# Wk's sums on VectorE late in the first chunk, and the next heads' operands earlier in the second pass

## The chip, the cores and the metric

The kernel runs on one core of a Trainium2 chip. The metric is the device time of one execution in microseconds. The kernel before has a median of 1039.54 us over three runs (1039.32, 1039.54, 1044.28).

## What is computed

A pre-norm layer on 2048 tokens of 512 features, in float32: a linear attention with 32 heads of 64, then a mixture of 8 experts with top 2.

```python
xn = layernorm(x)
q = relu(xn @ Wq); k = relu(xn @ Wk); v = xn @ Wv          # 512 -> 2048, 32 heads of 64
kv = einsum('bhsd,bhse->bhde', k, v)
key_sum = k.sum(over tokens)
out = (q @ kv) / clip(q @ key_sum, 1e-6)                   # per head
x = x + out @ Wo + bo
xn2 = layernorm(x)                                         # experts: H = 352
x = x + sum over the token's 2 best experts of gate * (silu(xn2 @ w1.T + b1) @ w2.T + b2)
```

## The kernel before

**Precision.** Each float32 matmul is three matmuls (`three`, lines 1928 to 1930) on operands split in a high and a low part: ScalarE casts the high part, VectorE subtracts it from the source for the low part (`lo`, line 1373). A product is ready for TensorE only when both have been made. Every engine runs its own queue in the order in which it is written, and engines wait for each other through semaphores; a waiting instruction holds all behind it on its engine.

**K projection and accumulation.** v is never projected. The kernel builds A^T = xn^T k (512 x 2048, in four chunks of 512 columns of k, `NC`), over 16 token tiles (`NT`), in the PSUM banks `pA`. K tiles come from `pK`. `kacc` collects k's sum over tokens.

- *First chunk* (tiles n = 0 to 15): per tile TensorE projects k of the next tile (12 matmuls, `project_k`), transposes one tile of xn, and accumulates (12 matmuls, `accumulate_at`). VectorE and ScalarE meanwhile do layernorm, the splits of xn, its transpose xnT and k, and one split of Wk a step (`split_wk`, table `WK_SPLIT`). `wk_in`, `wk2_in` and `t_raw` are staging areas in SBUF of four 512-column units each.
- *Groups* (g = 0 to 7): chunks 1 and 2 of k, for two tiles at a time, come from seven products instead of eight (the Winograd form of Strassen's scheme), from sums of Wk's quarters and sums of xnT's halves. Wk's sums (eight units of 128x512) are made once: by GpSimd in four instructions of 128x1024 (lines 662 to 668). The sums of xnT are `raw_sum`, split by `sum_hi` and `sum_lo`; the first group's stand ahead of `act_group` and `dve_group`, behind chunk 0. Chunk 2's k is stored to HBM as `k2`.
- *Second pass* (j = 0 to 7): k2 is loaded again and accumulated for chunk 2, two accumulations a turn. Between them lies the work of one pair of heads j: `pe_kv(j)` multiplies A^T's block (`at_hl`) with Wv, and `pe_m(j)` the block-diagonal of the result (`bd_hi`, `bd_lo`) with Wo. Their operands come from `act_operands` and `act_pair` on ScalarE (wv_hi, wo_hi, at_hl, ks_hl), `pool_operands` on GpSimd (wv_lo, wo_lo) and `dve_pair` on VectorE (low halves of at_hl and ks_hl). TensorE's turn: `pe_kv(j)`, accumulation of tile 2j-1 of k2, `pe_m(j)`, accumulation of tile 2j. `put_at(1)` copies chunk 1's finished A^T out of `pA` in turn 0; the second accumulation of that turn waits for it (`at_act`, `at_dve`).
- *Loads in the second pass* go through SyncE's one queue, in this order for pairs 4 to 7: k2 tile 2n, k2 tile 2n+1, Wv and Wo of pair n. The load of k2 tile i waits until the sum of tile i-4 (`kacc_done`) frees its buffer; Wk's last chunk (1 MB) goes ahead of pair 3.
- Then chunk 3 runs like chunk 0 (`pe_chunk`), the q projection and output product follow, and the experts.

Of the kernel before, what the change touches and what calls it, by code (L numbers as in the profile page):

```python
# [67 lines left out]
def block_kernel(nc, x, Wq, Wk, Wv, Wo, bo, gate_w, gate_b, gbias, w1, b1, w2, b2, out):  # L68
# [171 lines left out]
    with ExitStack() as ctx:  # L240
# [169 lines left out]
        WK_SPLIT = tuple((n, n + 2) for n in range(2, 14))  # L410
        wk_units = lambda n: [u for m, u in WK_SPLIT if m == n]
# [35 lines left out]
        def _(sp):  # L447
# [4 lines left out]
            for g in range(4):  # L452
# [5 lines left out]
                if g == 0:  # L458
# [6 lines left out]
            sp.dma_start(wk2_in[:, :].rearrange("p (f n) -> p f n", f=FB),  # L465
                         Wk[:, 2 * CW:3 * CW].rearrange("(f p) n -> p f n", p=P)).then_inc(s_wk, 16)
            sp.wait_ge(wk_lo_ready, FB)
            load_wk(1)
            def load_wq(c):
# [165 lines left out]
        def _(pool):  # L635
# [23 lines left out]

            two = lambda a, h: a[:, 2 * h * CW:2 * (h + 1) * CW]  # L660
            pool.wait_ge(s_wk, 32)
            pool.tensor_tensor(two(t_raw, 0), two(wk2_in, 0), two(wk_in, 0), ALU.subtract).then_inc(t_step, 1)
            pool.wait_ge(t_step, 1)
            pool.tensor_tensor(two(t_raw, 1), two(wk2_in, 1), two(t_raw, 0), ALU.subtract).then_inc(t_step, 1)
            pool.tensor_tensor(two(wk2_in, 0), two(wk2_in, 1), two(wk2_in, 0), ALU.subtract).then_inc(t_step, 1)
            pool.wait_ge(t_step, 3)
            pool.wait_ge(wk_lo_ready, 2 * FB)
            pool.tensor_tensor(two(wk_in, 1), two(t_raw, 1), two(wk_in, 1), ALU.subtract).then_inc(t_step, 1)
# [211 lines left out]
        def _(act):  # L880
            def split_wk(u, n):
                if n < FB:
                    act.wait_ge(s_block[n], 16)
                elif n >= 4 * FB + 2:
                    act.wait_ge(s_wk, 48)
                else:
                    act.wait_ge(s_wk, 32)
                    if u < 2 or u >= 10:
                        act.wait_ge(t_step, 4 if u < 2 else u // 2 - 4)
# [66 lines left out]
            def split_k2(i):  # L956
# [3 lines left out]
                else:  # L960
                    act.wait_ge(s_block[i % 4], 16 * (i // 4 + (1 if i % 4 < 2 else 2)))
# [27 lines left out]
            for n in range(NT):  # L989
                if n > 0:  # L990
                    split_k(n, n % 2)
                for u in wk_units(n):
                    split_wk(u, u)
                if n + 1 < NT:
                    act.wait_ge(xn_ready, n + 2)
# [71 lines left out]
            def act_group(g):  # L1067
# [3 lines left out]
                right_hi(g)  # L1071
                sum_hi(g, 4)
                if g > 0:
                    split_xn(n, 2 * g, 0)
# [16 lines left out]
            for k in (2, 1, 3):  # L1091
                sum_hi(0, k)
# [5 lines left out]
            for j in range(8):  # L1098
# [4 lines left out]
                act_bd(j)  # L1103
# [1324 lines left out]
```

## Time and profile before

| | |
|---|---|
| profiled execution, its own time | 1038.22 us |
| its span, first to last instruction | 1036.2 us |
| median of three timed runs | 1039.54 us |
| TensorE (PE) busy | 994.3 us, 96% |
| VectorE (DVE) busy | 745.3 us, 72% |
| ScalarE (ACT) busy | 518.4 us, 50% |
| GpSimd (POOL) busy | 289.0 us, 28% |

Busy shares are over the whole span, and TensorE's count overlapping matmuls, so its gaps must be looked for in a timeline. The page also cuts the span in 40 slices of 26 us; TensorE's row reads

```profile
PE   9899899997769999999999999999999989999998
```

in tenths, so that the only low stretch is slices 10 to 12 (233 to 311 us), in the second pass. Chunk 0 runs from the start to some 113 us, the groups to 234 us, the second pass to 319 us.

### The profile page before, as it was taken

Reading aid. Unit: us, or ns where it says so; the run is one execution under the profiler, and the core shown is the slowest. Engines: PE = TensorE matmul, PEld = TensorE weight load, DVE = VectorE, ACT = ScalarE, POOL = GpSimd, SP = SyncE. Lnnn points to the kernel's source line nnn. Section 1 sums busy time; section 2 is a strip of 40 time slices with the busy share of each in tenths; the row PEclk is TensorE's granted clock in tenths of the full one; section 3 lists DMA queues with packets and bytes.
Section 4 is the critical chain, followed back from the end, with each engine's and each line's share of the span. In section 5 each row is a group of like instructions: output and inputs, shape, how many; then the busy total and the mean of one; then the engine's idle time right before and its main releaser. Section 6 shows DMA issues by size and latency. Waiting matters only on the chain.

```text
span 1036.2 us, 17405 instructions
## 1 busy us (share of the span) xinstructions
PE 994.3 (96%) x4981; PEld 831.3 (80%) x4982; DVE 745.3 (72%) x1646; ACT 518.4 (50%) x1354; POOL 289.0 (28%) x433
## 2 busy tenths in 40 slices
PE   9899899997769999999999999999999989999998
PEld 7678688886657888888788888888888879899896
DVE  7988787877786566766788787887887665444453
ACT  4445423335554455865555555555555863434342
POOL 1210000012230000230432223322233555655554
PEclk9999999999999999999999999999999999999999
DMA  8000500104231003233212111111204735555553
GB/s 296 1 0 12 213 28 34 41 21 142 92 91 62 21 21 122 82 115 127 80 42 42 50 41 50 42 51 47 45 31 159 212 115 100 102 104 101 102 113 47
DMA packets 50898, 82.76 MB, mean 80 GB/s; under 512 B 6537, under 2 KB 19002, under 8 KB 50722
## 3 DMA queue, kind: packets, MB, share of 16 engines
q1 hardware_dynamic: 41042, 63.38, 19.3%
q0 software_dynamic: 9808, 18.79, 9.7%
q8 instruction: 24, 0.39, 0.2%
q14 instruction: 24, 0.20, 0.1%
HBM read 56.81 MB, written 27.17 MB: 81 GB/s over the span
## 4 chain that ended last, share of the span: by engine, by line
PE 85%; DVE 8%; ACT 5%; issue 1%; DMA 1%; SPq 0%; POOL 0%; ACTq 0%; DVEq 0%; POOLq 0%
PE pK L1928 15%; PE pK L1930 15%; PE pK L1929 15%; PE pX L1928 5%; PE pX L1930 5%; PE pX L1929 5%; PE pA L1928 5%; PE pA L1930 5%; PE pA L1929 5%; PE pA L2132 3%; PE pT L2342 2%; PE pT L2010 2%; PE pX L2360 1%; DVE ks_hl L1373 1%; DVE at_hl L1556 1%
## 5 line engine op out<-in xcount | busy, mean ns | idle before, releaser
L1139 ACT ACTIVATE qs<-q,nrec 128x64 f32<-128x64 f32 x512 | 129.6, 335 | 88.9 <-DVE nrec L1658 86.4
L657 POOL TENSOR_TENSOR wv_lo<-wv_in,wv_hi 128x512 fp32r<-128x512 f32 x12 | 15.4, 1287 | 354.5 <-ACT wo_hi L1010 354.5
L1928 PE MATMUL pA<-k_hi,xn_hi 128*128 128x512 f32 x256 | 101.5, 396 | 0.9 <-DVE k_lo L1393 0.6
L1928 PE MATMUL pK<-wq_hi,xnT_hi 128*128 128x512 f32 x256 | 100.4, 392 | 0.0
L1929 PE MATMUL pA<-k_lo,xn_hi 128*128 128x512 f32 x256 | 100.0, 391 | 0.0
L1930 PE MATMUL pA<-k_hi,xn_lo 128*128 128x512 f32 x256 | 99.9, 390 | 0.0
L1930 PE MATMUL pK<-wq_hi,xnT_lo 128*128 128x512 f32 x256 | 99.9, 390 | 0.0
L1929 PE MATMUL pK<-wq_lo,xnT_hi 128*128 128x512 f32 x256 | 99.7, 389 | 0.0
L1928 PE MATMUL pX<-m_hi,qsT_hi 128*128 128x512 f32 x240 | 99.1, 413 | 0.0
L1930 PE MATMUL pX<-m_hi,qsT_lo 128*128 128x512 f32 x240 | 94.2, 392 | 0.0
L1929 PE MATMUL pX<-m_lo,qsT_hi 128*128 128x512 f32 x240 | 93.7, 390 | 0.0
L1651 DVE TENSOR_TENSOR qs<-q,ksum 128x512 f32<-128x512 f32 x64 | 52.9, 827 | 54.5 <-ACT q L1133 54.5
L791 POOL DMA_INDIRECT out<-y,slot_token x38 | 65.9, 1733 | 69.4 <-DVE y L1894 42.3
L1928 PE MATMUL pK<-wk_hi,xnT_hi 128*128 128x512 f32 x192 | 76.3, 397 | 6.4 <-DVE xnT_lo L1373 3.9
L1929 PE MATMUL pK<-wk_lo,xnT_hi 128*128 128x512 f32 x192 | 74.9, 390 | 0.0
L1930 PE MATMUL pK<-wk_hi,xnT_lo 128*128 128x512 f32 x192 | 74.9, 390 | 0.0
L1133 ACT ACTIVATE q<-pK 128x512 f32<-128x512 f32 x64 | 38.1, 596 | 67.5 <-PE pK L1930 67.5
L1315 ACT ACTIVATE hT<-pX,b1T 128x128 f32<-128x128 f32 (+1 forms) x117 | 34.0, 362 | 72.0 <-PE pX L2360 64.1
L912 ACT CAST xn_hi<-xn 128x512 fp32r<-128x512 f32 x64 | 39.5, 617 | 50.8 <-PE pA L1930 50.8
L1928 PEld LDWEIGHTS pA<-k_hi,xn_hi 128*128 128x128 f32 x256 | 48.3, 189 | 11.5 <-DVE xn_lo L1373 0.8
L1373 DVE TENSOR_TENSOR gT_lo<-pT,gT_hi 128x512 fp32r<-128x512 f32 x39 | 27.0, 691 | 41.7 <-ACT gT_hi L1301 41.7
L1373 DVE TENSOR_TENSOR xn_lo<-xn,xn_hi 128x512 fp32r<-128x512 f32 x64 | 46.1, 720 | 14.9 <-ACT xn_hi L912 14.9
(314 smaller groups left out, 2603.0 us busy)
## 6 DMA issues: line engine op xcount, KB each, us to landing
w_in<-in_ffn_w SPq DMA_DIRECT2D x22, 256.0 KB, 3.6
w_in<-in_ffn_w SPq DMA_DIRECT2D x8, 704.0 KB, 7.2
xn<-in_attn_hidden_states SPq DMA_DIRECT2D x16, 256.0 KB, 6.3
wv_in<-in_attn_Wv SPq DMA_DIRECT2D x16, 256.0 KB, 2.9
wo_in<-in_attn_Wo SPq DMA_DIRECT2D x16, 256.0 KB, 3.1
xnT_dram<-xnT SPq DMA_DIRECT2D x4, 1024.0 KB, 9.6
wk_in<-in_attn_Wq SPq DMA_DIRECT2D x4, 1024.0 KB, 6.1
x_in<-in_attn_hidden_states SPq DMA_DIRECT2D x16, 256.0 KB, 2.6
```

The costliest lines, as they stand in the source:

```text
L791: pool.indirect_dma_start(out, bass.IndirectOffsetOnAxis(slot_token[:, i:i + 1].bitcast(U32), 0), rows, None, bounds_check=T - 1, oob_is_e ...
L912: nc.scalar.copy(xn_hi[:, b * D:(b + 1) * D], xn[:, ds(t * D, D)]).then_inc(xn_hi_ready, 1)
L1133: nc.scalar.activation(q[:, b * CW:(b + 1) * CW], pK[:, b * 512:(b + 1) * 512], ACT.Relu).then_inc(q_ready, 1)
L1139: i = nc.scalar.activation(qs[:, s], q[:, s], ACT.Copy, scale=nrec[:, b * HC + h:b * HC + h + 1])
L1315: last = nc.scalar.activation(hT[0:w, b * P:(b + 1) * P], pX[0:w, b * P:(b + 1) * P], ACT.Silu, bias=b1T[0:w, ds(b * E + e, 1)])
L1373: return nc.vector.tensor_tensor(dst, src, f(hi), ALU.subtract)
L1651: nc.vector.tensor_tensor(qs[:, b * CW:(b + 1) * CW], q[:, b * CW:(b + 1) * CW], ksum[:, c * CW:(c + 1) * CW], ALU.mult).then_inc(qk_ready, 1)
L1928: nc.tensor.matmul(dst, lhs[0], rhs[0], start=start, stop=False)
L1929: nc.tensor.matmul(dst, lhs[0], rhs[1], start=False, stop=False)
L1930: return nc.tensor.matmul(dst, lhs[1], rhs[0], start=False, stop=stop)
L2010: nc.tensor.matmul(pT[:, 0:256], w[:, b * D + i * P:b * D + (i + 1) * P], at_hl[:, i * 256:(i + 1) * 256], start=i == 0 and w is wv_hi, st ...
L2132: i = nc.tensor.transpose(pA[:, (2 + b) * 512 + j * P:(2 + b) * 512 + (j + 1) * P], qs[:, b * CW + j * P:b * CW + (j + 1) * P], ident[:, :])
```

## The change

In the first chunk GpSimd's four instructions go. VectorE makes the eight sums, 128x512 each, in `wk_sum`, by a table `WK_SUMS` of (step, sum): one at steps 8, 9 and 12, three at 13, two at 14. The table `WK_SPLIT` of (step, unit) changes with it: up to step 7 as before, then units 10 and 11 at steps 10 and 11, 12 and 13 at step 13, 14 and 15 at step 14. SyncE loads chunk 1 of Wk ahead of chunk 2, which now reports to `s_block[0]`. The first group's sums are made at step 15 of the first chunk, ahead of the split of xn's tile 16, and `right` and sum 4 with them. In the second pass the operands of pair j+1 are made on ScalarE and VectorE directly behind bd of pair j, ahead of `put_at(1)` and of the splits for the turn's other accumulation.

```diff
@@ -407,8 +407,9 @@
             at_ = (e * HB + hb) * D
             return bank[0:w], w, w2_to[0:w, at_:at_ + D]
 
-        WK_SPLIT = tuple((n, n + 2) for n in range(2, 14))
-        wk_units = lambda n: [u for m, u in WK_SPLIT if m == n]
+        WK_SPLIT = ((2, 4), (3, 5), (4, 6), (5, 7), (6, 8), (7, 9), (10, 10), (11, 11), (13, 12), (13, 13), (14, 14), (14, 15))
+        WK_SUMS = ((8, 0), (9, 1), (12, 2), (13, 3), (13, 4), (13, 5), (14, 6), (14, 7))
+        at_step = lambda table, n: [u for m, u in table if m == n]
 
         def wk_raw(u):
             if u < 2:
@@ -462,10 +463,10 @@
             sp.dma_start(bo_b[:, :], bo.partition_broadcast(P)).then_inc(s_small, 16)
             sp.dma_start(gb_b[:, :], gate_b.partition_broadcast(P)).then_inc(s_small, 16)
             sp.dma_start(gb2_b[:, :], gbias.partition_broadcast(P)).then_inc(s_small, 16)
-            sp.dma_start(wk2_in[:, :].rearrange("p (f n) -> p f n", f=FB),
-                         Wk[:, 2 * CW:3 * CW].rearrange("(f p) n -> p f n", p=P)).then_inc(s_wk, 16)
             sp.wait_ge(wk_lo_ready, FB)
             load_wk(1)
+            sp.dma_start(wk2_in[:, :].rearrange("p (f n) -> p f n", f=FB),
+                         Wk[:, 2 * CW:3 * CW].rearrange("(f p) n -> p f n", p=P)).then_inc(s_block[0], 16)
             def load_wq(c):
                 sp.dma_start(wk_in[:, :].rearrange("p (f n) -> p f n", f=FB),
                              Wq[:, c * CW:(c + 1) * CW].rearrange("(f p) n -> p f n", p=P)).then_inc(s_wq[c], 16)
@@ -657,16 +658,6 @@
                 pool.tensor_tensor(wv_lo[:, b], wv_in[:, b], f(wv_hi[:, b]), ALU.subtract).then_inc(wv_lo_ready, 1)
                 pool.tensor_tensor(wo_lo[:, b], wo_in[:, b], f(wo_hi[:, b]), ALU.subtract).then_inc(wo_lo_ready, 1)
 
-            two = lambda a, h: a[:, 2 * h * CW:2 * (h + 1) * CW]
-            pool.wait_ge(s_wk, 32)
-            pool.tensor_tensor(two(t_raw, 0), two(wk2_in, 0), two(wk_in, 0), ALU.subtract).then_inc(t_step, 1)
-            pool.wait_ge(t_step, 1)
-            pool.tensor_tensor(two(t_raw, 1), two(wk2_in, 1), two(t_raw, 0), ALU.subtract).then_inc(t_step, 1)
-            pool.tensor_tensor(two(wk2_in, 0), two(wk2_in, 1), two(wk2_in, 0), ALU.subtract).then_inc(t_step, 1)
-            pool.wait_ge(t_step, 3)
-            pool.wait_ge(wk_lo_ready, 2 * FB)
-            pool.tensor_tensor(two(wk_in, 1), two(t_raw, 1), two(wk_in, 1), ALU.subtract).then_inc(t_step, 1)
-
             for n in (*range(NPOOL), *range(NP - 4, NP)):
                 pool_operands(n)
 
@@ -882,11 +873,13 @@
                 if n < FB:
                     act.wait_ge(s_block[n], 16)
                 elif n >= 4 * FB + 2:
-                    act.wait_ge(s_wk, 48)
+                    act.wait_ge(s_wk, 32)
+                elif 4 <= u < 8:
+                    act.wait_ge(s_wk, 16)
+                elif u in (8, 9):
+                    act.wait_ge(s_block[0], 32)
                 else:
-                    act.wait_ge(s_wk, 32)
-                    if u < 2 or u >= 10:
-                        act.wait_ge(t_step, 4 if u < 2 else u // 2 - 4)
+                    act.wait_ge(t_step, u + 7 if u < 2 else u - 9)
                 src = wk_in[:, u % FB * CW:(u % FB + 1) * CW] if n < FB or n >= 4 * FB + 2 else wk_raw(u)
                 nc.scalar.copy(wk_hi[:, u * CW:(u + 1) * CW], src).then_inc(wk_hi_ready, 1)
 
@@ -958,7 +951,7 @@
                 if i < 2:
                     act.wait_ge(k2_ready, 2 * NG)
                 else:
-                    act.wait_ge(s_block[i % 4], 16 * (i // 4 + (1 if i % 4 < 2 else 2)))
+                    act.wait_ge(s_block[i % 4], 16 * (i // 4 + (1 if i % 4 == 1 else 2)))
                 act.wait_ge(a_done, n - 1)
                 nc.scalar.activation(k_hi[:, i % 2 * CW:(i % 2 + 1) * CW], k2_of(i), ACT.Relu).then_inc(k_hi_ready, 1)
 
@@ -989,8 +982,13 @@
             for n in range(NT):
                 if n > 0:
                     split_k(n, n % 2)
-                for u in wk_units(n):
+                for u in at_step(WK_SPLIT, n):
                     split_wk(u, u)
+                if n == NT - 1:
+                    for k in (2, 1, 3):
+                        sum_hi(0, k)
+                    right_hi(0)
+                    sum_hi(0, 4)
                 if n + 1 < NT:
                     act.wait_ge(xn_ready, n + 2)
                 split_xn(n + 1, (n + 1) % NT, (n + 1) % 2)
@@ -1068,9 +1066,9 @@
                 n = NT + 2 * g
                 if g > 0:
                     split_c(n - 1)
-                right_hi(g)
-                sum_hi(g, 4)
                 if g > 0:
+                    right_hi(g)
+                    sum_hi(g, 4)
                     split_xn(n, 2 * g, 0)
                 act.wait_ge(prod_done, 7 * g + 1)
                 nc.scalar.copy(p1[:, :], pK[:, 0:512]).then_inc(p1_ready, 1)
@@ -1088,8 +1086,6 @@
                     for k in (2, 1, 3):
                         sum_hi(g + 1, k)
 
-            for k in (2, 1, 3):
-                sum_hi(0, k)
             for u in range(2):
                 split_wk(u, 4 * FB + u)
             for g in range(NG):
@@ -1101,16 +1097,16 @@
                 split_xn(n, tile2(2 * j), 0)
                 act_part(j)
                 act_bd(j)
+                if j == 3:
+                    at_ready(2)
+                if j < 7:
+                    act_operands(j + 1, (j + 1) % 2, 32 * ((j + 1) // 2) + 32)
+                    act_pair(j + 1, (j + 1) % 4)
                 if j == 0:
                     put_at(1)
                 split_k2(2 * j + 1)
                 split_xn(n + 1, tile2(2 * j + 1), 1)
                 act_m(j)
-                if j == 3:
-                    at_ready(2)
-                if j < 7:
-                    act_operands(j + 1, (j + 1) % 2, 32 * ((j + 1) // 2) + 32)
-                    act_pair(j + 1, (j + 1) % 4)
                 if 3 <= j < 7:
                     split_wk(NT - 7 + j, 4 * FB + j - 1)
                 if j == 6:
@@ -1412,6 +1408,21 @@
             def sub(out, a, b, op=ALU.subtract):
                 return nc.vector.tensor_tensor(out, a, b, op)
 
+            def wk_sum(i):
+                if i == 0:
+                    dve.wait_ge(s_wk, 16)
+                    dve.wait_ge(s_block[0], 32)
+                dve.wait_ge(t_step, i)
+                if i == 6:
+                    dve.wait_ge(wk_lo_ready, 2 * FB)
+                unit = lambda a, n: a[:, n * CW:(n + 1) * CW]
+                h = i % 2
+                out, a, b = ((unit(t_raw, h), unit(wk2_in, h), unit(wk_in, h)),
+                             (unit(t_raw, 2 + h), unit(wk2_in, 2 + h), unit(t_raw, h)),
+                             (unit(wk2_in, h), unit(wk2_in, 2 + h), unit(wk2_in, h)),
+                             (unit(wk_in, 2 + h), unit(t_raw, 2 + h), unit(wk_in, 2 + h)))[i // 2]
+                sub(out, a, b).then_inc(t_step, 1)
+
             left = lambda t: xnT[:, t * D:t * D + HALF]
             right = lambda t: xnT[:, t * D + HALF:(t + 1) * D]
 
@@ -1456,9 +1467,8 @@
                 if g > 0:
                     split_c(n - 1)
                     add_k(1, n - 1, 1)
-                right_lo(g)
-                sum_lo(g, 4)
-                if g > 0:
+                    right_lo(g)
+                    sum_lo(g, 4)
                     split_xn(n, 2 * g, 0)
                 dve.wait_ge(prod_done, 7 * g + 2)
                 dve.wait_ge(p1_ready, g + 1)
@@ -1535,8 +1545,20 @@
                 if n > 0:
                     split_k(n, n % 2)
                     add_k(0, n, n % 2)
-                for u in wk_units(n):
+                for u in at_step(WK_SUMS, n):
+                    wk_sum(u)
+                for u in at_step(WK_SPLIT, n):
                     split_wk(u, u)
+                if n == NT - 1:
+                    for k in (1, 2):
+                        raw_sum(0, k)
+                    sum_lo(0, 2)
+                    sum_lo(0, 1)
+                    raw_sum(0, 3)
+                    raw_sum(0, 4)
+                    sum_lo(0, 3)
+                    right_lo(0)
+                    sum_lo(0, 4)
                 split_xn(n + 1, (n + 1) % NT, (n + 1) % 2)
                 if n + 2 < NT:
                     split_xnT(n + 2, n + 2, n % 2)
@@ -1604,13 +1626,6 @@
                             dve_m(pair)
                 put_at(c)
 
-            for k in (1, 2):
-                raw_sum(0, k)
-            sum_lo(0, 2)
-            sum_lo(0, 1)
-            raw_sum(0, 3)
-            raw_sum(0, 4)
-            sum_lo(0, 3)
             for u in range(2):
                 split_wk(u, 4 * FB + u)
             for g in range(NG):
@@ -1624,14 +1639,14 @@
                 add_k2(2 * j)
                 dve_kvT(j)
                 dve_bd(j)
+                if j < 7:
+                    dve_pair(j + 1, (j + 1) % 4, (j + 1) % 2)
                 if j == 0:
                     put_at(1)
                 split_k2(2 * j + 1)
                 split_xn(n + 1, tile2(2 * j + 1), 1)
                 add_k2(2 * j + 1)
                 dve_m(j)
-                if j < 7:
-                    dve_pair(j + 1, (j + 1) % 4, (j + 1) % 2)
                 if 3 <= j < 7:
                     split_wk(NT - 7 + j, 4 * FB + j - 1)
                 if j == 6:
```

## Rows read from the trace of the kernel before

**Rows 1.** Who TensorE waited for, whole span: total us, times, longest.
```profile
PE pT L2010 <- DVE ks_hl L1373: 18.8, 8, 2.7
```
**Rows 2.** Timeline of GpSimd, 22 to 60 us: start, duration, instruction, idle before.
```profile
26.47 2.41 POOL L662 TENSOR_TENSOR t_raw<-wk_in 128x1024 f32<-128x1024 f32 x1 [22.88 <-DMA wk_in<-in_attn_Wk]
...
51.74 2.69 POOL L668 TENSOR_TENSOR wk_in<-t_raw,wk_in 128x1024 f32<-128x1024 f32 x1 [17.56 <-DVE wk_lo L1373]
```
**Rows 3.** Timeline of VectorE, 22 to 60 us.
```profile
31.88 2.85 DVE L1373 TENSOR_TENSOR xn_lo<-xn,xn_hi 128x512 fp32r<-128x512 f32 x1
...
52.28 2.69 DVE L1373 TENSOR_TENSOR xnT_lo<-xnT,xnT_hi 128x512 fp32r<-128x512 f32 x1
```
**Rows 4.** Timeline of TensorE, 22 to 76 us: transposes of three tiles.
```profile
22.69 0.60 PE L1943 MATMUL pT<-ident,xn 128*128 128x128 f32 x4
...
69.97 0.60 PE L1943 MATMUL pT<-ident,xn 128*128 128x128 f32 x4
...
75.89 0.60 PE L1943 MATMUL pT<-ident,xn 128*128 128x128 f32 x4
```
**Rows 5.** Timeline of VectorE, 98 to 116 us.
```profile
100.20 0.68 DVE L1373 TENSOR_TENSOR wk_lo<-wk_in,wk_hi 128x512 fp32r<-128x512 f32 x1
...
109.69 0.42 DVE L1413 TENSOR_TENSOR s_raw<-xnT 128x256 f32<-128x256 f32 x1
110.14 0.42 DVE L1413 TENSOR_TENSOR s_raw<-s_raw,xnT 128x256 f32<-128x256 f32 x1
```
**Rows 6.** Timeline of TensorE and ScalarE, 102 to 116 us.
```profile
102.79 0.39 PE L1928 MATMUL pK<-wk_hi,xnT_hi 128*128 128x512 f32 x1
...
114.38 0.57 ACT L1076 COPY p<-pK 128x512 f32<-128x512 f32 x1
...
115.09 0.47 PE L1928 MATMUL pK<-wk_hi,s_hi 128*128 128x512 f32 x1 [1.26 <-DVE xnT_lo L1373]
```
**Rows 7.** Timeline of VectorE, second pass, turns 0, 1 and 7.
```profile
237.71 0.28 DVE L1564 TENSOR_TENSOR ksum<-pT,part 128x128 f32<-128x128 f32 x1
...
239.24 1.29 DVE L1409 COPY at<-pA 128x512 f32<-128x512 f32 x2
...
243.26 1.16 DVE L1556 TENSOR_TENSOR at_hl<-at,at_hl 128x512 fp32r<-128x512 f32 x1 [0.21 <-ACT ks_hl L1014]
...
245.62 0.68 DVE L1507 SCALAR_TENSOR_TENSOR k_lo<-k_in,k_hi 128x512 fp32r<-128x512 f32 x1
...
251.87 0.69 DVE L1513 SCALAR_TENSOR_TENSOR kacc<-k_in,kacc 128x512 f32<-128x512 f32 x1
...
311.49 0.28 DVE L1564 TENSOR_TENSOR ksum<-pT,part 128x128 f32<-128x128 f32 x1
```
**Rows 8.** Timeline of ScalarE, second pass, turn 0.
```profile
238.75 1.07 ACT L924 COPY at<-pA 128x512 f32<-128x512 f32 x2
...
241.37 0.62 ACT L1009 CAST wv_hi<-wv_in 128x512 fp32r<-128x512 f32 x1
```
**Rows 9.** Timeline of TensorE: turn 0, m(7), and chunk 3's first projection.
```profile
240.63 0.47 PE L1928 MATMUL pA<-k_hi,xn_hi 128*128 128x512 f32 x1 [0.34 <-issue]
...
313.13 0.47 PE L1928 MATMUL pX<-wo_hi,bd_hi 128*128 128x512 f32 x1 [0.98 <-DVE bd_lo L1373]
...
319.37 0.39 PE L1928 MATMUL pK<-wk_hi,xnT_hi 128*128 128x512 f32 x1
```
**Rows 10.** Timeline of SyncE's queue: the Wo load of pair 3.
```profile
253.98 0.50 SPq L477 DMA_DIRECT2D wo_in<-in_attn_Wo  x1
```
**Rows 11.** DMA issues, 253.8 to 256 and 264.8 to 265.5 us: KB, us to landing.
```profile
wo_in<-in_attn_Wo SPq DMA_DIRECT2D x1, 256.0 KB, 5.8
...
wo_in<-in_attn_Wo SPq DMA_DIRECT2D x1, 256.0 KB, 3.7
```
**Rows 12.** Busy time by stretch: length, PE, PEld, DVE, ACT, POOL, granted clock, DMA, GB/s.
```profile
254.00:256.00 2.00, 0.02 (x1) 0.05 (x1) 2.00 (x3) 0.53 (x2) 1.69 (x2) 0.93 0.97 288
256.00:258.00 2.00, 2.00 (x9) 2.00 (x10) 1.64 (x3) 0.00 (x0) 0.00 (x0) 0.50 1.05 384
```

## The prediction

> **What bounds the kernel now.** I read the page's busy shares first: TensorE is nearly always busy, so only a gap on TensorE is worth time. Then the table of who TensorE waits for. Its longest entry is the start of a pair's K-V product (`pe_kv`), which waits 18.8 us in 8 waits for `ks_hl`, the last operand that VectorE makes [rows 1]. Then the timelines of the two stretches that the change touches, engine by engine.
>
> First chunk: GpSimd makes Wk's sums from 26.47 on (three in a row) and at 51.74 [rows 2]. Beside them VectorE's 128x512 subtractions last 2.85 and 2.69 [rows 3], where the same operation takes 0.68 with GpSimd idle [rows 5]. TensorE pays: its transposes for one tile go from 22.69 to 69.97 in seven steps, and an undisturbed step is 75.89-69.97 = 5.92 [rows 4]. 47.28-7x5.92 = **5.84 us** are lost there.
>
> Second pass (eight pairs j, each with accumulation A, product m(j), accumulation B): a turn has 24 matmuls for A and B, 3 for m and 9 small ones. At (319.37-313.13)/27 = 0.231 a matmul [rows 9], and an estimated 1.1 for the small ones, the floor is near 7.3; the mean turn is (311.49-237.71)/7 = 10.5 [rows 7]. So the wait looks removable. What makes it is the question of the next part.
>
> **The change, part by part.** Times are the old trace's, before any shift.
>
> *1. GpSimd's sums go.* Nothing then slows VectorE up to 60 us. It has the same work per tile there as in the step of 5.92 that [rows 4] shows, so TensorE keeps 5.92: **-5.84**. The Wk loads only swap their order on SP's queue; the first user waits for chunk 1, which now comes first: 0.
>
> *2. Eight sums of 128x512 on VectorE.* At steps 8, 9 and 12 one sum takes the place of one split (0.60 from start to start): 0. Step 13 gets three sums and two splits where one split stood. A sum that waits for the one before starts 0.03 after its end (s_raw: 109.69+0.42, next at 110.14 [rows 5]), so 0.72. From 100.20 [rows 5], two steps of 0.72, then sum, split, split and xn_lo at 0.60 put xnT_lo at 104.04, done 104.73. TensorE's projection of tile 15 wants it at 102.79 [rows 6]: stall 2.0, with the restart 2.1. ScalarE stalls too, since its split of unit 13 is queued in front of xn_hi, xnT and k_hi of tile 14 and waits for the fourth sum (100.9); but these are four operations of 0.5 to 0.7, done by 103.8, and VectorE stays the later. Step 14 gets two sums and two splits; nine operations behind 104.04 give k_lo of tile 15 at 110.3, just when accumulation 15 may start.
>
> *3. The first group's sums before xn_lo of tile 16.* Before, the third product starts at 115.09, when ScalarE's copy p1 (114.38+0.57 [rows 6]) is done. Now raw sum 1 starts at 110.76, behind kacc; ScalarE casts its first sum at 111.73 and, waiting once for raw sum 3, is through all five half-width casts at 114.4; xn_hi and two wk_hi at 0.51 put p1 at 115.94, done 116.51, and TensorE starts at 116.65. All that follows hangs on this: parts 2 and 3 together cost 116.65-115.09 = **+1.56**. If these operations hid wholly it would be 0; if the stall of 2.1 stayed in full beside the old 1.3 of [rows 6], 3.4.
>
> First chunk: -5.84+1.56 = **-4.3** (-5.8 to -2.4).
>
> *4. Operands of pair j+1 straight behind bd(j).* They now run before k_lo, xn_lo, kacc of accumulation 2j+1 and m_lo, on both in-order queues. Call K(j) the start of ksum and W(j+1) the start of wv_hi. ScalarE's operation behind bd starts at 238.75 with K(0) = 237.71 [rows 7, 8]: W = K+1.04. From W, at_hl's low half follows at +1.89 (241.37 to 243.26), and VectorE's next operation at +4.25 (245.62) [rows 7, 8]; in that lie GpSimd's lower halves beside it (1.16 for an operation that takes 0.68 elsewhere), which stay. Then seven operations of 0.60 (k_lo, xn_lo, kacc, m_lo, and k_lo, xn_lo, kacc of the next) bring K(j+1) = W+8.45. So the turn is 8.45+1.04 = **9.5**, with wk_lo (j of 3 and up) 10.1. It is a loop of VectorE and ScalarE: TensorE's wait does not go, it is shared with a new one for bd_lo.
>
> *5. Loads.* Pair j+2 is loaded behind a load on SP's queue that waits for kacc of accumulation 2j+1, and that kacc is now behind the operands: its end is W(j+1)+4.25+1.2+0.69 = W+6.14. For pair 3, with Wk's 1 MB between, kacc ends at 252.56 [rows 7], wo is issued at 253.98 [rows 10] and lands 5.8 later [rows 11]: 7.2 behind kacc. For pair 4 it is 3.7 [rows 11], and without Wk's issue (0.5) some 0.9 pass before wo is issued: 4.6, an estimate from these rows. So W(3) = W(2)+13.4 and W(j+2) = W(j+1)+10.7 from there: ScalarE waits for data that it never waited for before, at 10.7 a turn against a mean of 10.5 today.
>
> The Trainium skill, "DMA: Bandwidth & Descriptors", section "Anatomy of one DMA" (written for GpSimd's path), has about 2.0 us fixed plus bytes at 436 GB/s. By it the three loads of 0.79 MB would be there 3.9 behind kacc, turns would be 10.0 to 10.1, and the sum below some 2.7 smaller.
>
> *6. The first turn.* `put_at(1)` stands behind the operands now. VectorE starts it at 238.75+4.25 = 243.0 and ends at 244.3 (before: 239.24+1.29), and accumulation B of j=0 waits for it: 244.39 against 240.63 [rows 7, 9], **3.76 of new stall**. TensorE has then been idle since 240.3 (240.63 less its 0.34 [rows 9]), 4.1 us. In the old trace the granted clock was 0.50 (1.2 GHz) from 256 to 258, behind a slice in which TensorE was busy for 0.02 of 2.00 us [rows 12]; I expect that behind this gap too. Twelve matmuls at half the clock cost at most 2.8, at none 0; I take 1.3. B ends at 248.5, k_hi and k_lo follow 0.9 later, K(1) is 251.25, W(2) 252.3, W(3) 265.7, W(7) 265.7+4x10.7 = 308.5. In j=6 ten operations of 0.60 follow (two are xnT_lo's): K(7) = W(7)+10.25 = 318.8. From ksum to chunk 3's first projection it is 319.37-311.49 = 7.88 [rows 7, 9]: it starts at 326.6, not 319.4: **+7.3**.
>
> Bounds of the second pass: no drop of the clock and loads never late give W(2) 251.0, W(3) 260.5, W(4) 270.0, W(7) 300.3, start 318.4: -0.9. Every load as late as pair 3's (5.8 for 3.7) adds 4x2.1: +15.7. I keep 3.7, as the loads of pairs 4 to 7 have no megabyte ahead of them either way.
>
> **Sum:** -5.84+1.56+7.3 = +3.0 us. On the profiled run's own 1038.22 that is 1041.2; the median of the runs shown is 1.3 above it (0.13%), so I forecast **1042.5 us**.
>
> **Rivals.** Half a per cent is 5.2 us, about what a measurement of this kernel tells from none.
> A. *Loads in time, no clock drop*: turns of 9.5 and 10.1, second pass -0.9, total -5.2: **1034.3**. For it: ScalarE leaves 9.49-6.14 = 3.35 for the loads, and 4.6 is not far off. Against: a landing of 3.7 alone is more than 3.35.
> B. *The wait really goes*: all 18.8 of [rows 1] and the first chunk's 4.3: **1016.4**. Against: it needs turns of 7.8, and VectorE's own loop is 9.5.
> C. *Slower*: the loads land like pair 3's in every turn. Place: W(4) to W(7); price 2.1 a turn, 8.4 together: **1050.9**; it decides from a landing of about 4.3 on. For it: the loads of a turn stand close behind each other on one queue. Against: only pair 3's, behind Wk's megabyte, took so long.
> D. *Slower*: GpSimd was not what slowed VectorE, so -5.84 never comes: **1048.4**. Against: two spans, both matching in place and length [rows 2, 3].
> E. *As forecast but no clock drop at 244*: **1041.2**, inside the forecast's own range. For it: the page's slices of the granted clock show no other drop, though gaps of like length follow in every turn. The Trainium skill, "TensorE: Matmul & The Clock Gate", section "What's actually happening", calls the throttled state the default, which activity releases; by that the longer gap makes a drop likelier than today's, and the time is 1042.5.
>
> **Chances.** Forecast with E: 0.72 (own range 1038 to 1045.5), A 0.10, B 0.04, C 0.07, D 0.07. Faster by over 0.5% (below 1034.3): half of A, B, and 0.01 of the rest, 0.10. Slower (above 1044.7): C, D and 0.07 of the forecast's upper end, 0.21. Within: 0.69. Range 1035 to 1047, from A's place to short of D.
>
> **What would show it.** In the changed profile: TensorE's steps of 5.92 from 23 to about 95 us and no subtraction over 0.7 there (1); one wait of about 2 us for xnT_lo at tile 15 (2); only some 0.8 of waiting ahead of the third product, for p1 (3); turns near 10.7 with two waits each, for bd_lo and for ks_hl (4), and wv_hi released by a load (5); a gap near 4 us ahead of accumulation B of j=0 and the granted clock at 0.5 behind it (6). Turns under 10, or wv_hi never waiting for a load, would prove the second half wrong; a first projection of chunk 3 that comes no later than before would overturn the forecast.

## The result, and the profile after

The changed kernel takes 1045.0 us (median of 20 runs, 1041.6 to 1047.2) against 1039.9 (20 runs, 1037.1 to 1044.3). The ratio is **1.0042, 95% interval [1.0031, 1.0054]**: 4.4 us slower (3.2 to 5.6), inside the 0.5% that the forecast called no change, though the interval's upper end lies just over it. The forecast was 1042.5, which is 3.0 us slower than before. The profiled execution of the changed kernel is 6.8 us longer than that of before (span 1043.0 against 1036.2). That pair overstates the change: the changed kernel's profiled execution (1044.91) is at its median, the one of before (1038.22) is 1.7 below its median. Most of the difference between 6.8 and the forecast's 3.0 is TensorE at half clock, as shown below. In the experiments a ratio is to the kernel before, timed on the same chip, with its 95% interval behind it; microseconds are the ratio times 1039.5.

First chunk, TensorE: start, duration, instruction, idle before it. The first three lines answer to [rows 4], the rest to [rows 6].
```profile
22.81 0.60 PE L1958 MATMUL pT<-ident,xn 128*128 128x128 f32 x4
...
64.28 0.60 PE L1958 MATMUL pT<-ident,xn 128*128 128x128 f32 x4
...
70.20 0.60 PE L1958 MATMUL pT<-ident,xn 128*128 128x128 f32 x4
...
99.10 0.50 PE L1943 MATMUL pK<-wk_hi,xnT_hi 128*128 128x512 f32 x1 [1.84 <-DVE xnT_lo L1369]
...
111.72 0.39 PE L1943 MATMUL pK<-wk_hi,s_hi 128*128 128x512 f32 x1
```
Seven steps take 64.28-22.81 = 41.47, 5.92 each; before, the same seven took 47.28. The projection of tile 15 waits 1.84 for xnT_lo. The third product has no wait in front of it, where it had 1.26.

VectorE in the same place: the sums and splits of step 13 ahead of that xnT_lo, whose end (98.36+0.69) is what TensorE's projection waited for.
```profile
94.51 0.68 DVE L1409 TENSOR_TENSOR t_raw<-wk_in,t_raw 128x512 f32<-128x512 f32 x1
95.22 1.42 DVE L1409 TENSOR_TENSOR wk_in<-wk_in 128x512 f32<-128x512 f32 x2
96.56 1.29 DVE L1369 TENSOR_TENSOR wk_lo<-t_raw,wk_hi 128x512 fp32r<-128x512 f32 x2
97.76 0.68 DVE L1369 TENSOR_TENSOR xn_lo<-xn,xn_hi 128x512 fp32r<-128x512 f32 x1
98.36 0.69 DVE L1369 TENSOR_TENSOR xnT_lo<-xnT,xnT_hi 128x512 fp32r<-128x512 f32 x1
```

Second pass, TensorE: the K-V products, the two marked stalls and chunk 3's first projection. They answer to [rows 9].
```profile
230.99 0.28 PE L2025 MATMUL pT<-at_hl,wv_hi 128*128 128x256 f32 x1
...
240.85 0.77 PE L1943 MATMUL pA<-k_hi,xn_hi 128*128 128x512 f32 x1 [4.07 <-issue]
...
254.43 0.36 PE L2025 MATMUL pT<-at_hl,wv_hi 128*128 128x256 f32 x1 [0.22 <-DVE ks_hl L1369]
...
267.72 0.55 PE L2025 MATMUL pT<-at_hl,wv_hi 128*128 128x256 f32 x1 [4.01 <-DVE ks_hl L1369]
...
278.52 0.35 PE L2025 MATMUL pT<-at_hl,wv_hi 128*128 128x256 f32 x1 [1.49 <-DVE ks_hl L1369]
...
318.40 0.74 PE L1943 MATMUL pX<-wo_hi,bd_hi 128*128 128x512 f32 x1 [3.30 <-DVE bd_lo L1369]
...
326.21 0.39 PE L1943 MATMUL pK<-wk_hi,xnT_hi 128*128 128x512 f32 x1
```
The pass starts 3.51 earlier than before (234.50 there) and ends 6.84 later: it grew by 10.35. The old pass had one place at half clock itself [rows 12]. Of its seven waits for ks_hl from 245 to 308 six last 2.64 to 2.69, and one of them has half clock behind it:
```profile
255.98 0.55 PE L2010 MATMUL pT<-at_hl,wv_hi 128*128 128x256 f32 x1 [2.68 <-DVE ks_hl L1373]
...
267.55 0.36 PE L2010 MATMUL pT<-at_hl,wv_hi 128*128 128x256 f32 x1 [2.68 <-DVE ks_hl L1373]
```
That turn takes 11.57, the five others 10.13 to 10.15: one drop of the clock costs the old pass 1.4, and the mean turn of 10.5 in the prediction is a turn of 10.14 and this drop.

What released ScalarE's wv_hi in the changed kernel's pass (start, duration, idle and releaser): pair 2, without a wait, then pairs 3, 4 and 5, answering to [rows 8].
```profile
249.92 0.62 ACT L1007 CAST wv_hi<-wv_in 128x512 fp32r<-128x512 f32 x1
...
263.27 0.62 ACT L1007 CAST wv_hi<-wv_in 128x512 fp32r<-128x512 f32 x1 [3.84 <-DMA wo_in<-in_attn_Wo]
...
274.04 0.62 ACT L1007 CAST wv_hi<-wv_in 128x512 fp32r<-128x512 f32 x1 [1.32 <-DMA wo_in<-in_attn_Wo]
...
284.85 0.62 ACT L1007 CAST wv_hi<-wv_in 128x512 fp32r<-128x512 f32 x1 [0.73 <-DMA wo_in<-in_attn_Wo]
```
Who TensorE waited for, against [rows 1]: the 18.8 us for ks_hl became 9.1, bd_lo went from 1.8 to 12.2, and 4.1 for put_at(1) ("issue") came.
```profile
PE pX L1943 <- DVE bd_lo L1369: 12.2, 7, 3.3
PE pT L2025 <- DVE ks_hl L1369: 9.1, 7, 4.0
PE pA L1943 <- issue: 4.1, 1, 4.1
```
Busy time by stretch (columns as in [rows 12]; the granted clock is the number before the last two): three places at half clock. A fourth begins at 267.72, behind the 4.01 of idle time above.
```profile
99.00:103.00 4.00, 3.90 (x11) 3.07 (x12) 3.96 (x8) 1.14 (x3) 0.00 (x0) 0.62 0.00 0
240.00:246.00 6.00, 5.15 (x12) 4.13 (x13) 3.15 (x6) 0.00 (x0) 0.00 (x0) 0.50 0.01 3
318.00:322.00 4.00, 3.60 (x9) 2.90 (x10) 2.83 (x6) 1.52 (x3) 0.00 (x0) 0.57 0.20 56
```

### The profile page after: what moved, and what is told of

It is laid out like the page before. It is cut to its first block, busy times and chain, and to the rows that moved or that the text cites. A ratio compares the mean times of both kernels' runs of the same rounds, so it can differ in the third digit from the quotient of the medians.

```text
span 1043.0 us, 17402 instructions
## 1 busy us (share of the span) xinstructions
PE 999.2 (96%) x4981; PEld 834.8 (80%) x4982; DVE 744.7 (71%) x1654; ACT 517.7 (50%) x1354; POOL 278.0 (27%) x429
## 4 chain that ended last, share of the span: by engine, by line
PE 83%; DVE 9%; ACT 3%; DMA 2%; issue 1%; SPq 0%; POOL 0%; POOLq 0%; DVEq 0%; ACTq 0%
PE pK L1943 15%; PE pK L1945 15%; PE pK L1944 15%; PE pX L1943 5%; PE pX L1945 5%; PE pX L1944 5%; PE pA L1943 5%; PE pA L1944 5%; PE pA L1945 5%; PE pA L2147 3%; PE pT L2357 2%; DMA wo_in<-in_attn_Wo 1%; PE pX L2375 1%; DVE ks_hl L1369 1%; DVE at_hl L1578 1%
## 5 line engine op out<-in xcount | busy, mean ns | idle before, releaser
L1945 PEld LDWEIGHTS pA<-k_hi,xn_lo 128*128 128x128 f32 x256 | 49.0, 192 | 10.8
L1944 PEld LDWEIGHTS pA<-k_lo,xn_hi 128*128 128x128 f32 x256 | 49.2, 192 | 9.7
```

What stands on the lines that cost most here:

```text
L1944: nc.tensor.matmul(dst, lhs[0], rhs[1], start=False, stop=False)
L1945: return nc.tensor.matmul(dst, lhs[1], rhs[0], start=False, stop=stop)
```

## Experiments

**1 and 2. One half of the change each.** The second pass's lines put back in their old order, and the kernel before with only those lines moved:
```diff
 # 1: changed kernel, both queues           # 2: kernel before, the opposite move
-                if j < 7:
-                    dve_pair(j + 1, (j + 1) % 4, (j + 1) % 2)
                 if j == 0:
                     put_at(1)
 ...
                 dve_m(j)
+                if j < 7:
+                    dve_pair(j + 1, (j + 1) % 4, (j + 1) % 2)
```


> The change with the second pass in its old order: only the first chunk's part (Wk's sums on VectorE, the first group's sums early). Theory A (GpSimd slowed VectorE; the stall at tile 15 puts TensorE at half the granted clock for some 3.5 us, which gives about 1.5 back): the kernel is 3.5 us faster than before, ratio about 0.9966, and projection 15 still starts near 99.1 with the clock at 0.50 behind it. The forecast's terms alone (-5.84+1.56, no clock drop): 4.3 faster, 0.9959. Rival D (GpSimd was not what slowed VectorE): no faster than before, 1.000 or more.

> The kernel before with only the second pass's new order (operands of pair j+1 straight behind bd(j), put_at(1) behind them). Theory A (the late put_at, loads on the path, and half clock behind two gaps, at accumulation B of j=0 and at m(7)): slower by 8 to 10.3 us, ratio 1.0077 to 1.0099. The forecast's term alone (one clock drop at 1.3): 7.3 slower, 1.0070. If the two parts work on each other (the changed first chunk made the second pass dearer), the second pass alone costs clearly less, 4.4 or below, 1.0042.

Measured: the first chunk alone 0.9971 [0.9955, 0.9987], 3.0 us faster; the second pass alone 1.0090 [1.0067, 1.0113], 9.4 slower. Each agrees with theory A, but the forecast's own terms (0.9959 and 1.0070) lie in the intervals too: these two runs don't size the clock's part. Their sum (+6.4) agrees with the change's +4.4 within the intervals. Rival D is out: with the sums off GpSimd the kernel is faster. No sign is seen that the halves work on each other, and one of them is a gain.

**3. put_at(1) ahead of the operands again**, nothing else:
```diff
+                if j == 0:
+                    put_at(1)
                 if j < 7:
                     dve_pair(j + 1, (j + 1) % 4, (j + 1) % 2)
-                if j == 0:
-                    put_at(1)
```


> The change with one thing back: put_at(1) ahead of the operands of pair 1 on both queues. Theory A: accumulation B of j=0 starts behind m(0) at about 237.1 instead of 240.85, no half clock there, ksum of j=1 at 244.8 instead of 248.9 and everything behind it 4.1 earlier: against the kernel before about +0.3 us, ratio 1.0003. Forecast's sizes (3.76 of stall and 1.3 of clock, of which VectorE's own loop keeps part): 3.0 less than the change. Rival (the loads are the whole loss, the late put_at is hidden behind them): as the change, 1.0042.

Measured: 1.0016 [1.0002, 1.0029], 2.7 us less than the change. That is nearest to the forecast's own sizes (3.0); theory A's 1.0003 is at the interval's edge and not excluded. The rival of a put_at hidden behind the loads (1.0042) is out. In its profile chunk 3's first projection stands at 323.05, 3.2 earlier than in the changed kernel, and kv(2) 4.8 earlier. TensorE, start, duration, idle, and the wait of ScalarE's wv_hi in the longest turn:
```profile
249.59 0.36 PE L2025 MATMUL pT<-at_hl,wv_hi 128*128 128x256 f32 x1 [0.23 <-DVE ks_hl L1369]
...
262.99 0.55 PE L2025 MATMUL pT<-at_hl,wv_hi 128*128 128x256 f32 x1 [4.12 <-DVE ks_hl L1369]
...
270.10 0.62 ACT L1007 CAST wv_hi<-wv_in 128x512 fp32r<-128x512 f32 x1 [2.11 <-DMA wo_in<-in_attn_Wo]
...
274.58 0.38 PE L2025 MATMUL pT<-at_hl,wv_hi 128*128 128x256 f32 x1 [1.84 <-DVE ks_hl L1369]
```
From 262.99 the turn takes 11.59 where the same turn of the changed kernel takes 10.80 (267.72 to 278.52). Half clock lasts longer in it (16 matmuls for 11), but that isn't what makes it long: TensorE waits 1.84 for ks_hl at its end. The load does. Pair 4's wo was issued at 265.52 and released wv_hi 4.58 later, where the changed kernel has 3.78 (270.26 to 274.04): the 0.8 of this turn. Experiment 4 has 17 matmuls at half clock in the same turn, a landing of 3.82, and a turn of 10.85. What the other 0.9 up to the projection is made of is not shown; this execution has two more places at half clock than the changed kernel behind 270. The first chunk has the same code as the changed kernel, but here the clock held:
```profile
98.00:104.00 6.00, 5.10 (x22) 4.24 (x23) 5.97 (x11) 2.54 (x5) 0.00 (x0) 1.00 0.02 7
```
and the third product stands where the forecast had it (116.65-5.84 = 110.81), behind the wait for p1 that the forecast had (0.8) and that the changed kernel's profile did not show:
```profile
110.81 0.47 PE L1943 MATMUL pK<-wk_hi,s_hi 128*128 128x512 f32 x1 [0.57 <-ACT p L1074]
```
From the projection of tile 15 to the product that waits for v_sum it is 113.32-98.90 = 14.42 here and 114.12-99.10 = 15.02 in the changed kernel: half clock over most of that projection cost 0.6 net, since TensorE would have waited for p1 anyway.

**4. The clock kept by dummy work** (transposes of the identity that nobody reads) in three gaps:
```diff
+                    if n == NT - 2:
+                        pe.wait_ge(bT_ready, 1)
+                        keep_clock(14, pX)       # ahead of the projection of tile 15
 ...
+                if j == 7:
+                    pe.wait_ge(m_lo_ready, 7)
+                    keep_clock(24, pX)           # ahead of m(7)
 ...
                 if j == 0:
+                    keep_clock(30, pT)           # ahead of accumulation B
```


> The change with dummy transposes of the identity on TensorE in three gaps: 14 ahead of the projection of tile 15, 30 ahead of accumulation B of j=0, 24 ahead of m(7). They write banks that are free then and change no result. Theory A (half clock behind the three gaps costs 1.5, 2.5 and 1.8): the granted clock stays at 1.0 there and the kernel is up to 5.8 us faster than the change, about -1 against the kernel before, ratio 0.999. If the clock's part is the 1.3 that the forecast gave: 3 slower than before, 1.003. If a half clock costs nothing on the path (other engines are later): as the change, 1.0042.

Measured: 1.0022 [1.0009, 1.0035], 2.1 less than the change, not 5.8, and the two intervals overlap a little. The value that goes with a clock's part of 1.3 (1.003) lies inside the interval. The clock was kept where the dummies stood, and was at half elsewhere. Accumulation B (first line; the dummies fill TensorE up to it), and three stretches of the same execution, 266 to 270, 293 to 296 and 304 to 307; in the changed kernel the last two were at 1.00:
```profile
240.11 0.47 PE L1943 MATMUL pA<-k_hi,xn_hi 128*128 128x512 f32 x1 [0.82 <-issue]
```
```profile
266.00:270.00 4.00, 4.00 (x13) 3.32 (x12) 3.42 (x9) 0.86 (x3) 0.00 (x0) 0.50 0.60 192
293.00:296.00 3.00, 3.00 (x11) 2.33 (x10) 1.24 (x2) 3.00 (x7) 1.91 (x2) 0.66 0.11 42
304.00:307.00 3.00, 3.00 (x9) 2.37 (x8) 1.34 (x2) 3.00 (x7) 2.01 (x2) 0.53 0.40 113
```
That the dummies moved the drops there is not shown: experiment 3, without dummies, has one at 291.72 too. In this execution chunk 3's first projection stands at 321.94, 4.3 earlier than in the changed kernel: 0.8 came up to kv(0), 2.5 at accumulation B and 1.6 behind m(7), less 0.5 between. So the first chunk gave 0.8 of its expected 1.5, for p1's wait came in its place. Why the timed runs gain only 2.1 stays open.

**5 and 6. Loads early**, alone and with put_at(1) first:
```diff
             load_k2(6)
+            next_pair(3)
             load_k2(7)
             load_wk(3)
-            next_pair(3)
             for n in range(4, 8):
                 load_k2(2 * n)
+                next_pair(n)
                 load_k2(2 * n + 1)
-                next_pair(n)
```


> The change with one order on SP's queue altered: pair n's two loads are issued ahead of the k2 load that waits for kacc of accumulation B (and pair 3's also ahead of Wk's megabyte). Theory A (the loads behind that kacc put ScalarE's wv_hi on the path): wv_hi never waits for a load, kv(2) to kv(3) takes 9.6 in place of 13.3, the other turns 9.5 and 10.1 in place of 10.7 to 10.9; the kernel is about 7 us faster than the change, 2.6 faster than before, ratio 0.9975. Rival (the loop of VectorE and ScalarE alone makes the turn; the loads land in its shade): turns stay at 10.7, ratio 1.0042 as the change. Rival (only pair 3's wait is the loads' doing): 3.7 less than the change, 1.0007.

> The loads early and put_at(1) ahead of the operands together. Theory A (two separate losses, they add up): turns of 9.5 and 10.1 and no stall ahead of accumulation B of j=0; 2.8 less than with the loads early alone, about 5.4 faster than before, ratio 0.9948. If the early loads already hide the late put_at: as with the loads early alone, 0.9975. In the trace the first projection of chunk 3 stands near 312.5, where the kernel before has it at 319.4.

Measured: 0.9966 [0.9952, 0.9980] and 0.9933 [0.9914, 0.9952]. The one order on SP's queue is worth 7.9 us of the change, and put_at another 3.4; both together are 7.0 us faster than before. The losses are separate and add up (2.7 alone, 3.4 on top). The rival of a turn that VectorE and ScalarE make by themselves at 10.7 is out, and so is the one that only pair 3's wait is the loads' doing (1.0007). With both, TensorE's K-V products of pairs 2 to 4:
```profile
249.62 0.36 PE L2025 MATMUL pT<-at_hl,wv_hi 128*128 128x256 f32 x1 [0.23 <-DVE ks_hl L1369]
...
259.14 0.36 PE L2025 MATMUL pT<-at_hl,wv_hi 128*128 128x256 f32 x1 [0.22 <-DVE ks_hl L1369]
...
268.67 0.36 PE L2025 MATMUL pT<-at_hl,wv_hi 128*128 128x256 f32 x1 [0.24 <-DVE ks_hl L1369]
```
Turns of 9.52 and 9.53: the loop of 9.5 that the prediction worked out, with no wv_hi that waits for a load.

**7 and 8. First chunk spread**: three sums and the last four splits of Wk moved behind xnT_lo (step 13) and the first group's rows (step 14), p1 ahead of the last two splits; 7 on top of 6, 8 with the old second pass.
```diff
-        WK_SUMS = (... (12, 2), (13, 3), (13, 4), (13, 5), (14, 6), (14, 7))
+        WK_SUMS = (... (12, 2), (13, 3), (14, 6))
+        WK_SUMS_LATE = ((13, 4), (13, 5), (14, 7))      # behind split_xnT / rows
+        WK_SPLIT_LATE = ((13, 12), (13, 13), (14, 14), (14, 15))
```


> As the one before, and in the first chunk five operations of steps 13 and 14 (three sums and four splits, less those that stay) moved behind xnT_lo of tile 15 and behind the rows of the first group, p1 ahead of the last two splits of Wk. Theory A (the stall at tile 15 comes only from what stands ahead of xnT_lo, and VectorE's whole work up to the first group's sums stays): no wait for xnT_lo at tile 15, but the third product gains only p1's place, 0.6 to 1.7 us; 6 to 7 faster than before, ratio 0.9935 to 0.994. If the stall of 1.85 is gone in full: 2.4 less than the one before, 0.9925.

> Only the first chunk's part, with the same spreading, and the second pass in its old order. Theory A: 0.6 to 1.7 us faster than the first chunk's part as it is, 3.6 to 4.7 faster than before, ratio 0.9955 to 0.9965. If the stall was all that the first chunk's part lost of its 5.84: 5.8 faster than before, 0.9944.

Measured: 0.9925 [0.9906, 0.9943] against 0.9933 without, and 0.9953 [0.9934, 0.9973] against 0.9971: 0.8 and 1.9 us, neither outside its interval. The wait for xnT_lo is gone and one of the same size stands a step later, in 8:
```profile
103.99 0.47 PE L1952 MATMUL pA<-k_hi,xn_hi 128*128 128x512 f32 x1 [1.80 <-DVE k_lo L1394]
```
VectorE's work up to there is the same, so the stall is moved and not removed.

**9 and 10. The second pass's lower halves on VectorE**, on top of 6 and of 7:
```diff
-NPOOL = 8
+NPOOL = 1
 ...
             def dve_pair(n, j, b):
-                dve.wait_ge(c_hi_ready, n + 1)
                 if NPOOL <= n < NP - 4:
+                    dve.wait_ge(operands_hi, n + 1)
                     lo(wv_lo ...); lo(wo_lo ...)
+                dve.wait_ge(c_hi_ready, n + 1)
```


> The loads early and put_at(1) ahead of the operands, and in the second pass the lower halves of Wv and Wo of pairs 1 to 7 made by VectorE (two 128x512 subtractions more for it in each turn) and not by GpSimd. Theory A (two engines on SBUF slow each other, as in the first chunk): at_hl's low half takes 0.68 in place of 1.15 and ks_hl's 0.28 in place of 1.35; VectorE's operation behind ks_hl comes 3.1 behind the start of wv_hi in place of 4.25, turns are 8.4 and 9.0 in place of 9.5 and 10.1; about 8 us less than with both of the orders alone, ratio near 0.9855. Rival (GpSimd's halves ran for nothing and VectorE gets two operations more): 7x1.2 = 8.4 slower than that, 1.0014.

> The same, with the first chunk's operations spread as well (the version with everything). Theory A: 0 to 1 us below the one before, ratio 0.9845 to 0.9855. If TensorE becomes the bound of the turn (27 matmuls at 0.231 and the small ones, near 7.3): no less than 0.9855 and waits for ks_hl gone.

Measured: **0.9857 [0.9830, 0.9884]**, 14.9 us faster than before, and 0.9866 [0.9838, 0.9894] with the spread. Theory A said 0.9855. One turn of VectorE in the kernel before (one line; at_hl is at 1.16 in [rows 7]), then ScalarE's wv_hi and VectorE in experiment 9:
```profile
244.34 1.35 DVE L1373 TENSOR_TENSOR ks_hl<-kacc,ks_hl 128x128 fp32r<-128x128 f32 x1
```
```profile
252.74 0.62 ACT L1007 CAST wv_hi<-wv_in 128x512 fp32r<-128x512 f32 x1
...
253.91 0.69 DVE L1369 TENSOR_TENSOR wv_lo<-wv_in,wv_hi 128x512 fp32r<-128x512 f32 x1 [0.71 <-ACT wo_hi L1008]
254.52 0.69 DVE L1369 TENSOR_TENSOR wo_lo<-wo_in,wo_hi 128x512 fp32r<-128x512 f32 x1
255.12 0.68 DVE L1579 TENSOR_TENSOR at_hl<-at,at_hl 128x512 fp32r<-128x512 f32 x1
255.73 0.28 DVE L1369 TENSOR_TENSOR ks_hl<-kacc,ks_hl 128x128 fp32r<-128x128 f32 x1
255.93 0.69 DVE L1517 SCALAR_TENSOR_TENSOR k_lo<-k_in,k_hi 128x512 fp32r<-128x512 f32 x1
```
The operation behind ks_hl comes 3.19 behind wv_hi, where it was 4.25. VectorE has two operations more and is through sooner. Turns are 8.43, and 9.04 with wk_lo (expected 8.4 and 9.0). The spread brings nothing here. In both, TensorE no longer waits for ks_hl in the second pass but for bd_lo, 0.9 to 1.5 a turn, so it is not yet the bound.

**11. The old order without GpSimd** (experiment 1 with the lower halves on VectorE).

> The first chunk's part of the change, the second pass in its old order, and the lower halves of Wv and Wo of pairs 1 to 7 on VectorE. Theory A (in the old order too the wait for ks_hl is made by the loop through the slowed operations): ks_hl is ready 1.1 earlier behind the start of wv_hi, turns 9.0 in place of 10.14; 8 us less than the first chunk's part alone, ratio 0.9894. Rival (in the old order TensorE waits for ks_hl at the end of VectorE's queue and two more operations there lengthen the turn): 10.14 or more, 0.997 or above. Against the version with the sooner operands (0.9857) this tells what the order itself is worth once GpSimd is out of the way.

Measured: 0.9923 [0.9904, 0.9942], 5 us less than experiment 1 where theory A said 8. Its K-V products, and the clock behind two of them:
```profile
249.86 0.39 PE L2026 MATMUL pT<-at_hl,wv_hi 128*128 128x256 f32 x1 [1.92 <-DVE ks_hl L1369]
...
260.85 0.39 PE L2026 MATMUL pT<-at_hl,wv_hi 128*128 128x256 f32 x1 [1.90 <-DVE ks_hl L1369]
...
270.26 0.39 PE L2026 MATMUL pT<-at_hl,wv_hi 128*128 128x256 f32 x1 [1.92 <-DVE ks_hl L1369]
```
```profile
250.00:253.00 3.00, 3.00 (x13) 2.71 (x14) 2.10 (x5) 0.62 (x3) 0.00 (x0) 0.56 1.06 382
260.80:263.80 3.00, 2.95 (x17) 2.65 (x18) 2.40 (x6) 0.86 (x3) 0.00 (x0) 1.00 0.39 131
```
Turns alternate: 9.41 at full clock, then 10.99 with half clock in it, three of each, behind gaps of the same 1.9. No wv_hi waits for a load. Theory A's turn of 9.0 did not come: it is 9.41 at full clock, and the 1.58 more in three turns lie on the path. In the profiles this pass is no shorter than experiment 1's (kv(1) to kv(7) 61.2 against 60.8), but the profiled execution of experiment 1 is the fastest of its twelve, 4.4 below their median, with no half clock in its second pass. Once GpSimd is out of the way the sooner operands, with put_at(1) first and the loads early, are worth some 6.9 us (0.9923 to 0.9857, measured on two chips).

**12. Dummies in the best version** (experiment 9 with 14 ahead of tile 15's projection and 18 ahead of m(7), placed as in 4).

> The loads early, put_at(1) first, lower halves on VectorE, and dummy transposes of the identity in the two gaps that are left over 1.8 us: 14 ahead of the projection of tile 15, 18 ahead of m(7). Theory A (each drop of the clock that is hidden behind no other wait costs what the slower matmuls take): no clock of 0.50 in 98 to 104 and 296 to 304, 0.6 and 1.8 less, up to 2.4 faster than without them, ratio about 0.9835. Rival (the drop only moves to the next gap, as in the four-gap pass of the changed kernel, where 2.1 came of the expected 5.8): 0.985 to 0.986.

Measured: 0.9851 [0.9828, 0.9874], 1023.3 us, against 0.9857 without. In the profile no drop is left in 98 to 104 or 296 to 304, as theory A has it: the same stretch without and with the dummies,
```profile
300.00:304.00 4.00, 4.00 (x13) 3.10 (x12) 1.69 (x3) 0.59 (x1) 0.00 (x0) 0.57 0.68 189
```
```profile
300.00:304.00 4.00, 4.00 (x19) 3.31 (x18) 1.75 (x3) 0.64 (x2) 0.00 (x0) 1.00 0.83 230
```
chunk 3's first projection at 304.7 against 306.9. But the profiled execution of experiment 9 (1026.3) is the slowest of its six. In the timed runs the difference is 0.6 us and not told from nothing: both theory A's 0.9835 and the rival's 0.985 to 0.986 lie in the interval. Whether dummies pay here stays open.

## Why the prediction was right or wrong

By its steps, times of the changed kernel's profile:

1. **GpSimd's sums, -5.84**: right. Seven steps are 5.81 shorter, and experiment 1 is a gain. The Trainium skill, "GPSIMD Engine Reference", section "Key points", says that GpSimd shares its SBUF interfaces with VectorE and contends with its instructions of two SBUF inputs; [rows 3] and experiment 9 agree (2.85 and 2.69 for 0.68; 1.16 for 0.68).
2. **Stall at tile 15, 2.0 (2.1 with restart)**: right, 1.84 (2.23 from start to start).
3. **The third product, +1.56**: right in place. It holds when the clock does: experiment 3 has the third product at the forecast's 110.81 and kv(0) at 230.21, which is 4.29 sooner than before, the forecast's 4.3. Here the half clock took its place; the first chunk's gain is 3.5 at kv(0). This step said nothing of the clock, and 0.6 of the 0.8 is the clock.
4. **A turn of 9.5 and 10.1**: right, shown bare in experiment 6: 9.53, and with wk_lo 10.11 (m(5) at 285.01 less m(4) at 274.90).
5. **Loads**: right. W(3)-W(2) = 263.27-249.92 = 13.35 for 13.4, then 10.8 a turn for 10.7; the first wait is 3.84, the rest 0.6 to 1.3. Pair 4's wv_hi is released 4.7 behind kacc's end (269.38), for 4.6. By the rule of the Trainium skill, "DMA: Bandwidth & Descriptors", section "Anatomy of one DMA", the estimate was 3.9, and turns of 10.0 to 10.1; the trace does not agree (the page has that rule for GpSimd's path, these loads are SyncE's). Rivals A (loads in time) and C (5.8 in every turn) fall with the measured 10.8, rival D with experiment 1.
6. **The first turn**: accumulation B at 240.85, where 244.39-3.51 = 240.88 was said; the gap is 4.1 and the clock 0.50 behind it, as expected. **The size failed: "Twelve matmuls at half the clock cost at most 2.8, at none 0; I take 1.3."** All twelve ran at half clock, 0.43 apart for 0.23, about 2.4.
7. **From W(7) on (the last part of step 6), 18.1**: it took 326.21-306.46 = 19.75. K(7) came as said (W(7)+10.3), but m(7) waits 3.3 for bd_lo and half clock follows over some eight matmuls. The forecast priced one drop and this one is the same thing again.

The profiled execution missed the sum by 6.84-3.0 = 3.8: 0.8 in the first chunk, 1.1 at accumulation B, 0.3 in the loads, 1.6 behind m(7). The term that was mis-sized is the clock: one drop at 1.3 where the profile has four, three of them on the path at 0.6, 2.4 and about 1.5 (the fourth, at 267.7, is hidden behind VectorE's loop). That is one execution, and drops differ between executions of one kernel (experiments 1, 3 and 5 have the same first chunk: the clock from 98 to 104 is 0.72, 1.00 and 1.00).

That the timed +4.4 lies nearer the forecast than the profile's 6.8 is partly luck. The kernel before has drops too, which the prediction left out: its executions in the experiments took 1036.5 to 1038.4 us where the granted clock of the whole span was 0.997 or 0.998, and 1041.6 to 1044.2 where it was 0.991. The profile that the sum was built on is one of the first kind, with a single drop. The median execution (0.996) probably holds more of them, and they cancel a part of the changed kernel's, which were priced too low. How large a part is not measured.

On rival E (no drop of the clock at all) [rows 12] had pointed the right way: what TensorE does behind one gap in the old trace it did here behind four.

Against rival B the prediction argued rightly that the wait for ks_hl could not simply go, but saw the cause only by half: two operations that GpSimd slows make a good part of the loop of 9.5 (8.4 without, experiment 9), and in the prediction they were something "which stay". They are worth 7.9 us (0.9933 to 0.9857), as much as the order of the loads.

## What to carry to other kernels

When operands are moved sooner on an in-order queue, follow what the moved-past operations release: here a load (7.9 us) and a copy out of PSUM (2.7), which together turned a gain into a loss. An operation given to GpSimd was not free here: beside it VectorE's operations with two SBUF inputs took 1.7 to 4.8 times as long. And a new gap on TensorE is priced with its length and with the matmuls behind it at half clock, as a range, since whether they run so differs between executions (behind gaps of 1.84 to 2.7 us it was seen both ways). For the same reason a single profile of either kernel can be 2 to 4 us from the median: look where in the timed runs it lies before a difference of two profiles is explained.

## What the runs showed of the hardware

- Taking two 128x512 subtractions over from GpSimd made VectorE's turn shorter by 1.1 us: it pays 1.2 for them, gets back 0.48 on at_hl and 1.07 on ks_hl, and it starts 0.7 sooner, while ScalarE still casts (1.17 behind wv_hi for 1.89).
- The granted clock fell to 0.50 behind gaps of 4.1, 4.0, 3.3 and 1.84 us in the changed kernel, but held behind three of 2.1 that follow each other 11 us apart. In experiment 11 equal gaps of 1.9 were followed by half clock every second time. In the kernel before one of six gaps of 2.6 to 2.7 was, and none of six in experiment 1's profile. With three gaps filled the clock was at half behind others of 4.1, 2.1 and 1.9 (experiment 4).
- Half clock shows as 128x512 matmuls 0.43 apart for 0.23. It costs the path nothing where the loads and VectorE make a turn longer than TensorE's slowed one (10.80 with 11 slow matmuls from 267.7, 10.85 with 17 in experiment 4, 10.68 to 10.94 with none), and nearly all of it where TensorE is the next to be late (1.6 behind m(7)).
- A load of 256 KB with the same two issues ahead of it released its reader 3.78, 3.82 and 4.58 us after its issue in three executions (pair 4's wo in the changed kernel, experiments 4 and 3), and the turn got longer by as much.
